# The last layer split in three: its weights folded into the output projection, its part in x2 computed between two stages

## The reference

```python
x = x + einsum('bct,bcd->bdt', x, w0[subjects])      # layer 0: a 32x32 matrix for each sequence
x = x + einsum('bct,bcd->bdt', x, w1[conditions])    # layer 1: the same with another table
x = x + attention(x)                                 # layer 2: see below
out = x + x @ W.T + s_b * ((x @ A_b.T) @ B_b.T)      # layer 3: W 256x256, adapter of rank 16, 8 adapters
```

## Time and profile before

| | us |
|---|---|
| time, median of 3 runs (lowest, highest) | 499.41 (495.37, 501.82) |
| the profiled execution: its time | 497.69 |
| its span, first to last instruction | 495.9 |
| TensorE / VectorE / ScalarE / GpSimd busy | 382.6 / 345.0 / 266.1 / 107.7 |
| mean granted TensorE clock, share of full | 0.904 |

### The profile page before, as it was taken

The page is one execution under the profiler, slowest core; times in us unless marked ns, Lnnn a source line. Parts: engine busy times, 40 slices in busy tenths (PEclk is TensorE's granted clock), DMA queues, the critical chain, the costliest instruction groups (busy, mean ns, idle before and its releaser), DMA issues.

```text
span 495.9 us, 16985 instructions
## 1 busy us (share of the span) xinstructions
PE 382.6 (77%) x6190; PEld 283.8 (57%) x6190; DVE 345.0 (70%) x1017; ACT 266.1 (54%) x977; POOL 107.7 (22%) x178
## 2 busy tenths in 40 slices
PE   1753777888875006969879999999899999987996
PEld 0342534444442004757767777777777777776785
DVE  6994277898889805647656677677777777765782
ACT  3302555666665105545645766666766676654662
POOL 5300043333334620211211221211211221220000
PEclk9855798999999555799989999999999999998999
DMA  3999122222212066788877768867878969875200
GB/s 111 386 399 385 44 79 74 73 78 72 78 55 81 21 140 169 154 163 172 191 191 168 163 169 171 169 153 165 186 173 160 191 173 162 180 188 128 71 24 23
DMA packets 68866, 73.57 MB, mean 148 GB/s; under 512 B 18190, under 2 KB 65326, under 8 KB 66528
## 3 DMA queue, kind: packets, MB, share of 16 engines
q1 hardware_dynamic: 61968, 39.38, 33.9%
q0 software_dynamic: 6864, 33.72, 25.0%
HBM read 70.83 MB, written 26.21 MB: 196 GB/s over the span
## 4 chain that ended last, share of the span: by engine, by line
PE 32%; DMA 18%; ACT 9%; issue 5%; DVE 1%; SPq 1%; ACTq 0%; DVEq 0%; POOLq 0%
PE probT_bank L1123 6%; ACT rope L608 6%; PE out_bank L1147 5%; DMA kvbuf<-new_scratch,winidx 5%; PE score_banks L1084 4%; PE keys_bank L1066 3%; DMA window<-value_scratch 3%; DMA value_scratch<-kvbuf 3%; PE score_banks L1079 3%; ACT window L599 3%; PE out_bank L1134 3%; DMA out<-early 3%; DMA kvbuf<-in_kv,winidx 2%; PE out_bank L1148 2%; PE out_bank L1141 2%
## 5 line engine op out<-in xcount | busy, mean ns | idle before, releaser
L608 ACT ACTIVATE rope<-score_banks,negm 128x176 f32<-128x176 f32 x256 | 102.0, 414 | 4.2 <-DVE negm L886 4.0
L886 DVE TENSOR_REDUCE negm<-score_banks 128x2 f32<-128x352 f32 x128 | 61.0, 518 | 35.1 <-PE score_banks L1084 34.4
L896 DVE TENSOR_SCALAR rope<-rope,rinv 128x176 f32<-128x176 f32 x256 | 69.6, 314 | 4.6
L624 ACT COPY early<-probT_bank 128x128 f32<-128x128 f32 x64 | 17.0, 266 | 88.4 <-PE probT_bank L1123 88.4
L1011 PE MATMUL probT_bank<-wts,x2T 128*128 128x512 f32 x128 | 63.1, 617 | 1.8 <-DVE early L732 1.8
L433 POOL DMA_INDIRECT new_scratch<-stage,rowidx x32 | 36.5, 1142 | 111.9 <-DVE stage L757 107.0
L903 DVE COPY rope<-probT_bank 128x512 f32<-128x512 f32 x64 | 44.3, 692 | 18.6 <-PE probT_bank L1103 14.9
L608 ACT ACTIVATION_READ_ACCUMULATOR rope<-score_banks,negm 128x1 f32 x256 | 54.3, 212 | 0.0
L1123 PE MATMUL probT_bank<-rope,window 128*32 128x64 f32 x2048 | 43.8, 226 | 6.3 <-issue 3.4
L599 ACT COPY window<-keys_bank 128x352 f32<-128x352 f32 x60 | 46.7, 779 | 1.5 <-PE keys_bank L1066 1.5
L1066 PE MATMUL keys_bank<-ident,kvbuf 88*128 88x88 f32 x240 | 32.8, 262 | 16.0 <-ACT window L599 13.9
(11 more groups left out here) (179 smaller groups left out, 705.4 us busy)
## 6 DMA issues: line engine op xcount, KB each, us to landing
value_scratch<-kvbuf SPq DMA_DIRECT2D x16, 704.0 KB
window<-value_scratch SPq DMA_DIRECT2D x16, 512.0 KB, 11.6
work<-in_x SPq DMA_DIRECT2D x16, 256.0 KB, 2.7
new_scratch<-window SPq DMA_DIRECT2D x2, 2048.0 KB, 12.0
out<-early SPq DMA_DIRECT2D x32, 128.0 KB, 5.8
window<-value_scratch SPq DMA_DIRECT2D x32, 96.0 KB, 8.6
new_scratch<-kvbuf SPq DMA_DIRECT2D x1, 2048.0 KB, 14.2
wts<-in_weights SPq DMA_DIRECT2D x1, 1280.0 KB, 8.2
```

The source lines that it names most:

```text
L608: ins = a.activation(prob[:, par, P_AT[h]:P_AT[h] + KEYS], psS[:, h, 0:KEYS], ACT.Exp, bias=negm[:, par, h:h + 1], accum_out=sums[:, par, ...
L886: v.tensor_reduce(negm[:, par, 2 * half:2 * half + 2], psS[:, 2 * half:2 * half + 2, 0:KEYS], axis=AX_X, op=ALU.max, negate=True).then_inc ...
L896: ins = v.tensor_scalar(prob[:, par, at], prob[:, par, at], rinv[:, par, h:h + 1], None, ALU.mult)
```

## The change

Layer 3's weights are multiplied by Wo once, on chip: `wo` becomes Wo^T (W + I)^T in place and `woA` is Wo^T A^T. After the tile stage, a loop over the 32 tiles computes x2's part of the output (4 matmuls a tile: two of 128 columns for the adapter's inner product, two of 256) into score banks; ScalarE copies the result over `xres`, and VectorE writes the masked inner product into `xa2`. Attention then only adds o's part: `project` is 2 matmuls of 128 columns and 2 of 256, `adapter` and `add3` are gone, `final` is 1 matmul of 256, `adapt_x2` adds the kept inner product, and `y_out` moves from ScalarE to VectorE, where it adds the kept part of x2. The masks, `admask` and W + I are computed ahead of the tile stage, since the new loop needs them. All scratch is taken from areas that are free by then. On the host Wo's layout changes.

```diff
 # ScalarE
+            for u in range(2):
+                act.wait_ge(s["fused"], u + 1)
+                a.copy(woA[:, u, :], psP[u][:, 256:384])
+            act.wait_ge(s["fused"], 2)
+            for u in range(2):
+                a.copy(wo[:, u, :], psP[u][:, 0:256]).then_inc(s["fused_kept"], 1)
+            for n in range(TILES):
+                act.wait_ge(s["x2_made"], n + 1)
+                a.copy(xres[:, n, :], psS[:, n % 2, 0:256]).then_inc(s["x2_kept"], 1)
...
 # VectorE: the block at L866 to L881 now stands behind L852, ahead of the first sumsq
...
+            def y_out(m, par):
+                dve.wait_ge(s["l3"], m + 1)
+                if not (isinstance(m, int) and m < 2):
+                    dve.wait_ge(s_out[par], (m - par) * 8)
+                v.tensor_tensor(ys[:, par, :], xres[:, bass.ds(m, 1), :].rearrange("p o f -> p (o f)"), psZ[:, 0:256],
+                                ALU.add).then_inc(s["y"], 1)
...
             def adapt_in(m):
-                dve.wait_ge(s["xa"], m + 1)
+                dve.wait_ge(s["wo"], m + 1)
+                wait_from(dve, s["l3"], m)
...
+            def adapt_x2(m):
+                dve.wait_ge(s["xa_part"], m + 1)
+                v.tensor_tensor(xam, xam, xa2[:, bass.ds(m, 1), :].rearrange("p o n -> p (o n)"), ALU.add).then_inc(s["xam"], 1)
...
 # VectorE, period
                 if par == 1 and not (known and m < 1):
                     adapt_in(m - 1)
+                if par == 0 and not (known and m < 2):
+                    y_out(m - 2, (k // 2) % 2)
                 probT_out(c, par)
+                if par == 1 and not (known and m < 1):
+                    adapt_x2(m - 1)
...
+            for n in range(TILES):
+                dve.wait_ge(s["x2_made"], n + 1)
+                v.tensor_tensor(xa2[:, n, :].rearrange("p (b t) -> p b t", b=SPT),
+                                psS[:, 2 + n % 2, 0:P].rearrange("p (b t) -> p b t", b=SPT),
+                                spread(admask[:, n * SPT:n * SPT + SPT], 2, ROWS), ALU.mult).then_inc(s["xa2_kept"], 1)
...
 # TensorE, behind the tile stage
+            pe.wait_ge(s["xcopy"], TILES)
+            for u in range(2):
+                for at, n, w in ((0, 256, w3T), (256, P, laT)):
+                    for f in range(2):
+                        ins = t_.matmul(psP[u][:, at:at + n], wo[:, f, P * u:P * u + P], w[:, f, :], start=(f == 0), stop=(f == 1))
+                ins.then_inc(s["fused"], 1)
+            for n in range(TILES):
+                wait_from(pe, s["x2_kept"], n - 1)
+                wait_from(pe, s["xa2_kept"], n - 1)
+                for f in range(2):
+                    t_.matmul(psS[:, 2 + n % 2, 0:P], laT[:, f, :], xres[:, n, P * f:P * f + P], start=(f == 0), stop=(f == 1))
+                for f in range(2):
+                    ins = t_.matmul(psS[:, n % 2, 0:256], xres[:, n, P * f:P * f + P], w3T[:, f, :], start=(f == 0), stop=(f == 1))
+                ins.then_inc(s["x2_made"], 1)
...
+                for u in range(2):
+                    t_.matmul(psZ[:, 256:256 + P], woA[:, u, :], oT[:, u, :], start=(u == 0), stop=(u == 1))
+                for u in range(2):
+                    ins = t_.matmul(psZ[:, 0:256], oT[:, u, :], wo[:, u, :], start=(u == 0), stop=False, skip_group_check=True)
                 ins.then_inc(s["wo"], 1)
...
             def final(m):
                 pe.wait_ge(s["xam"], m + 1)
-                for f in range(2):
-                    t_.matmul(psZ[:, 0:256], x3T[:, P * f:P * f + P], w3T[:, f, :], start=(f == 0), stop=False)
-                t_.matmul(psZ[:, 0:256], xam, lbT, start=False, stop=True).then_inc(s["l3"], 1)
+                t_.matmul(psZ[:, 0:256], xam, lbT, start=False, stop=True, skip_group_check=True).then_inc(s["l3"], 1)
...
+            pe.wait_ge(s["fused_kept"], 2)
+            pe.wait_ge(s["x2_kept"], TILES)
+            pe.wait_ge(s["xa2_kept"], TILES)
             scores(0, 0, 0, 0)
```

More of the change, by code:

```diff
@@ L141, in build @@
         ident = sb("ident", [P, P])
-        work2 = sb("work2", [P, 3072])
+        work = sb("work", [P, 6144])
+        e1, work2 = work[:, 0:3072], work[:, 3072:]
+        xa2 = work[:, 1408:1408 + TILES * P].rearrange("p (t n) -> p t n", t=TILES)
         wts = sb("wts", [P, sum(W_PARTS)])
         w_at = [sum(W_PARTS[:k]) for k in range(len(W_PARTS))]
-        wqkvT, woT, w3T, laT = (wts[:, a:a + n].rearrange("p (c n) -> p c n", c=2) for a, n in zip(w_at[:4], W_PARTS))
+        wqkvT, wo, w3T, laT = (wts[:, a:a + n].rearrange("p (c n) -> p c n", c=2) for a, n in zip(w_at[:4], W_PARTS))
         lbT = wts[:, w_at[4]:]
+        woA = sb("adapted_wo", [P, 2, P])
         mixw = work2[:, 0:2048].rearrange("p (l d t) -> p l d t", l=2, t=TILES)
@@ L237, in build @@
         x2T = sb("x2T", [P, 2, 2, P])
-        early = sb("early", [P, 4, 2, 384])
+        early = e1.rearrange("p (a b n) -> p a b n", a=4, b=2)
         sq, qn, rc, rs = (early[:, k] for k in range(4))
@@ L625, in heads_out @@
                        headsT.rearrange("p (s u t) -> p u s t", s=2, u=2)).then_inc(s["ote"], 1)
[L627 to L632, removed]
             def period(o, k):
@@ L640, in period @@
                 units = k % CPG < 2 and not (known and group >= GROUPS)
-                if par == 0 and not (known and m < 2):
-                    y_out(m - 2, (k // 2) % 2)
                 if not first:
@@ L852, in _ @@
             v.tensor_copy(winidx[:].rearrange("p k g -> p (k g)"), turned_wins[0:GR]).then_inc(s["winidx"], 1)
[L853 to L864, removed]
             dve.wait_ge(s["masks"], 2)
@@ L881, in _ @@
             ins.then_inc(s["w3_plus_one"], 1)
+            for j in range(2):
+                sumsq(j, j)
+                norm(j, j)
+            part2(0, True, True)
+            part2(1, True, True)
+            base = ch.base + ch.n
+            with dve.Fori(2, PAIRS - 1) as i:
+                ch.start(base + (i - 2) * 10)
+                part2(i, True, True)
+                assert ch.n == 10
+            ch.start(base + 10 * (PAIRS - 3))
+            part2(PAIRS - 1, False, True)
             def maxes(c, par, half):
@@ L903, in probT_out, with adapt_in @@
                 v.tensor_copy(probT[:, par, 0:512], psP[0][:, :]).then_inc(s["pte0"], 1)
[L905 removed]
+            def y_out(m, par):
[4 more added lines that the diff above has]
+                                ALU.add).then_inc(s["y"], 1)
+            def adapt_in(m):
                 dve.wait_ge(s["wo"], m + 1)
[L907 to L911 removed]
+                wait_from(dve, s["l3"], m)
                 v.tensor_tensor(xam.rearrange("p (b t) -> p b t", b=SPT),
@@ L926, in period @@
                     adapt_in(m - 1)
+                if par == 0 and not (known and m < 2):
+                    y_out(m - 2, (k // 2) % 2)
                 probT_out(c, par)
+                if par == 1 and not (known and m < 1):
+                    adapt_x2(m - 1)
                 if not last:
[L929 to L933, removed]
+                    for half in range(2):
+                        normalise(c + 1, 1 - par, half)
             dve.wait_ge(s["qte"], TILES)
@@ L952, in _ @@
                 period(COUPLES // 8 - 1, k)
-            add3(TILES - 1)
+            y_out(TILES - 2, 0)
             adapt_in(TILES - 1)
+            adapt_x2(TILES - 1)
+            y_out(TILES - 1, 1)
         @block.tensor
@@ L1162, in period @@
                     unit(group, (k // CPG + 1) % 2, 2 * (k % CPG))
-                if par == 1 and not (known and m < 1):
-                    adapter(m - 1)
                 probs_T(c, par)
```

22 lines of the change are left out of this document (4 added, 18 removed).

## The result

The changed kernel takes 528.13 us (median of 4 runs, 519.19 to 533.3), against 500.62 for the kernel before (4 runs, 495.37 to 504.81). The ratio is 1.0477, with a 95% interval of 1.0245 to 1.071: slower. It goes by the fast runs alone (519.19 and 526.18 of the changed kernel, mean 522.7; 495.37, 499.41 and 501.82 of before, mean 498.9), since the other three were in a slower state. The forecast was 517, range 507 to 528: the direction was right, and 522.7 lies inside the range, though the median of all four runs lies just past its upper end. The profiled execution of the changed kernel is its fastest run, 519.19 us with a span of 517.4; it stands 21.5 us over the profiled execution of before (497.69), where the working gave 19.7. That pair is what the rows show; what the other runs have on top of it is in no trace.

A forecast was written before the change was run, and what follows sets the result against it. VectorE bounds the tile stage, a key wait the gap, the exponentials' loop and TensorE attention's periods. Later attention 35.2, first couples -4, steady attention -10.2 and tail -1.3 sum to +19.7 us on 497.69: 517, range 507 to 528.

The forecast's parts named there:

- What bounds the kernel: Gap between tile stage and attention: a wait for patched keys, hiding only some 13 of the loop's 48 us.
- The block: Masks, admask and W + I ahead of the tile stage: nothing covers them, so the stage ends 8.4 us later.
- The loop: In the gap: 1.36 us a tile, 43.5 for 32, copies hidden; with the rest, attention starts 35.2 us later.
- the cold array: Start of the loop in the gap: low clock costs 2 us, bounds 0 and 8.
- Steady groups: Attention, every four couples: -0.66 us a group of 17.9, -10.2 us for some 15.5 groups.
- The floor by the exponentials' loop: Attention: scores, maxima, exponentials and next scores form a loop; no period without keys goes under about 3.7 us.
- A: Rival: attention is TensorE's after all, so all 29 us of its saving come back; 498.6 us, chance 0.12.
- B: Rival: attention gains nothing, final waiting each time and the longer project always on the path; 527.6 us, chance 0.15.
- C: Rival: each loop tile waits for its copies, 0.6 us more a tile, 19 us in all; 536 us, chance 0.05.
- D: Rival: the block hides ahead of the tile stage, where VectorE idles 15.0 us; 509 us, chance 0.04.
- The first couples: Start of attention: a warm array and earlier transfers take back 4 of 4.3 us, between 1 and 6.
- The tail: Last project to last output copy: one handoff fewer and 0.93 us less of matmuls, -1.3 us, bounds -0.5 and -2.

The follow-up runs named there:

- no_loop: The changed kernel without the loop over x2 (xa2 set to zero, its part of the output not computed): 503.25 us, against 497.8 for the kernel before.
- loop_only: The kernel before with the loop added in the gap, results unused, VectorE's block reordered but still behind the tile stage: 515.94 us, ratio 1.0329.
- block_back: The changed kernel with masks, admask and W + I put back behind the tile stage, W + I and admask first: 514.39 us, ratio 1.0263.
- y_first: The changed kernel with y_out ahead of the next couple's maxima on VectorE in even periods: 523.82 us, ratio 1.0489.

## Why the prediction was right, and where not

- **What bounds the kernel.** The gap is a wait for the keys and hides only some 13 us of a loop of 48: shown by no_loop (12.04 us of wait) and by loop_only, where the loop alone moves the first scores by 23.6 us and costs 17.
- **The block:** 8.4 us forecast, 8.33 taken, 7.9 of them at the first sumsq, and block_back gives 5.6 back at the first scores. Nothing covered it, as said.
- **The loop:** 48.2 us forecast (2.7, 43.5 and 2 for the cold array), 45.6 measured. A tile takes 1.31 us for 1.36: the copies hide behind the next tile's matmuls as said, and the matmuls were a little cheaper than their price. The cold array cost only 1.0 us, all in the folded weights. Attention began 31.55 us later, not 35.2.
- **Steady groups:** -0.66 us forecast, -0.54 measured. By periods: even with keys +0.42 (forecast +0.43), odd with keys -0.84 (-0.81), odd without -0.44 (-0.35, with final waiting 0.61 us for adapt_x2), even without +0.32 (+0.07). The last was the error: the longer project fits in the idle 0.36 us only if it can start on time, and it waits for y_out, which stands behind the maxima; y_first takes 0.26 of the 0.32 away. The group that was read, 17.92 us, was not the usual one: most of before take 17.65. The floor by the exponentials' loop held for this change, with 3.68 us for the odd period, but it isn't as firm as the prediction has it: before's own trace has three periods of 3.53.
- **The rivals.** A (all of TensorE's saving returns) falls with the groups, which give 0.54 us and not the 1.86 that it needs. B (no saving in the groups) falls with the same 0.54, though its 527.6 is near the median of all runs. C (handoffs in the loop) falls with the 1.31 us of a tile, D (the block hides) with the first sumsq at 66.48.
- **The first couples:** -4 forecast on top of the steady saving; the measured -5.4 holds two groups and an odd period without keys, 1.5 us of steady saving, so that 3.9 are left. (The prediction counts the ninth period as one of 4.96 us with keys; by its place it is the odd one without, 4.12.) The size was right and the reason half wrong: not the clock, which fell to 0.55 at once, but, as far as the runs tell, the DMAs' head start.
- **The tail:** -1.3 forecast. From the last project (511.73) to the start of the last y_out (514.75) are 3.02 us for 4.37.
- **The term that was furthest out** is the -10.2 us of attention, and with it the sentence "what ScalarE's wait for that DMA costs today, VectorE's costs then". Of the 10.2, 8.9 belong to the 13.5 groups between the tenth and the last couple; there the pair gave back 3.2. Of the 5.7 us between, 1.6 are the mis-sized even period, and 4.1 are stalls. The stall on VectorE cost 10.7 us for a wait of 7.80, the one on ScalarE 4.3 for 4.79, so the sentence doesn't hold for a single wait.
- **Luck in the number.** Attention began 3.65 us earlier than forecast and gave back 5.7 less: the two errors go against each other, and 19.7 came out near the pair's 21.5.
- **What stays open.** With four buffers in both kernels the ratios differ by 4.5%, some 22 us, near the 19.7 of the working, and with two by 4.8%. By how much the store wait alone sets the changed kernel back against the one before lies within the interval of the ratio.

## What to carry to other kernels

Work moved into a gap is free only up to the length of the wait that the gap is; price the rest as path, and check what the gap's end depends on (here the block ahead of the tile stage pushed both ends). A saving inside a loop counts only as far as the slowest recurrence in it and the transfers behind it: when a period shortens, look at the buffers whose reuse waits for a store, and try more buffers first. Here that edit alone, on the kernel before, gave 1.4% and the lowest ratio of all, while the change with block, buffers and order put right stayed at 1.0047. A wait for a DMA that moves to another engine costs what stands behind it there.

## What the hardware showed unexpectedly

A 128 KB store that lands in a median of 5.8 us (before) and 7.1 us (after) took up to 14.2 and 16.3 us, and one landing of 15.99 us stopped VectorE for 7.80. TensorE's granted clock was 0.98 through the folded weights and 41.9 us of dense matmuls and still full in the first score mask at 220.27 (0.48 us). Over the 12.8 us from 220.20 it was 0.55, though the engine was busy 10.1 of them: the mask at 223.67, behind 2.40 us of idling for the exponentials, already takes 0.77 us.
